# Retention block between two feed-forwards, one core: the last block in two tiles of 128 tokens, and a new order of fill and drain

## The reference, cut to what matters

```python
x = x + 0.5 * ffn(layernorm(x))          # FFN1
x = x + retention(layernorm(x))          # RET, 8 heads of 32, chunks of 64 in the reference
x = x + 0.5 * ffn(layernorm(x))          # FFN2

def ffn(x):                              # x_prev is x moved down by one token
    xr = mu_r * x + (1 - mu_r) * x_prev
    xk = mu_k * x + (1 - mu_k) * x_prev
    r = sigmoid(xr @ W_r.T)
    return r * (square(relu(xk @ W_k.T)) @ W_v.T)

def retention(x):                        # per head, state S carried from chunk to chunk
    q, k, v = x @ Wq, x @ Wk, x @ Wv
    o = ((q @ k.T) * D) @ v + (q * decay_q) @ S
    S = decay_s * S + (k * decay_k).T @ v
    return concat_heads(o) @ Wo
```

## Time and profile before

| | us |
|---|---|
| median of 3 runs | 339.76 |
| lowest, highest | 339.11, 339.87 |
| the profiled execution | 338.8 |
| its span, first to last instruction | 336.9 |

### The profile page before, as it was taken

How to read it: one execution, slowest core, us unless ns; L and a number is a source line. 1 busy time by engine, 2 the same in 40 slices (tenths; PEclk the granted TensorE clock), 3 DMA queues, 4 the chain that set the end, 5 groups by cost and what they waited for, 6 DMA issues and landing times.

```text
span 336.9 us, 11291 instructions
## 1 busy us (share of the span) xinstructions
PE 322.3 (96%) x4260; PEld 302.4 (90%) x4260; DVE 297.0 (88%) x696; ACT 210.5 (62%) x422; POOL 135.1 (40%) x242
## 2 busy tenths in 40 slices
PE   4979999999999999999999999999999999999975
PEld 4869899999999999999899999989999998989874
DVE  4989899999999999899999989999897979888954
ACT  2877556775757586674758567475857555374362
POOL 4386165608163451706245270715424154221130
PEclk9999999999999999999999999999999999999999
DMA  7610010102001020201102020100000010000001
GB/s 232 247 35 31 4 34 0 34 5 62 4 2 63 2 65 3 65 2 27 41 3 64 2 63 2 53 16 32 2 19 17 2 35 7 26 4 31 34 2 62
DMA packets 11556, 12.08 MB, mean 36 GB/s; under 512 B 1008, under 2 KB 11120, under 8 KB 11504
## 3 DMA queue, kind: packets, MB, share of 16 engines
q1 hardware_dynamic: 11072, 11.18, 10.4%
q10 hardware_dynamic: 432, 0.20, 0.2%
HBM read 7.18 MB, written 4.19 MB: 34 GB/s over the span
## 4 chain that ended last, share of the span: by engine, by line
PE 88%; DVE 4%; issue 3%; ACT 2%; POOL 1%; DMA 1%; ACTq 0%; DVEq 0%; POOLq 0%
PE psum L964 39%; PE psum L956 24%; PE psum L948 7%; PE psum L1035 5%; PE psum L1067 5%; PE psum L1054 3%; PE psum L1025 2%; PE psum L1080 2%; PE psum L1157 1%; DMA ident<-in_ident 1%; ACT xn L344 1%; DVE stats L624 1%; PE psum L1161 1%; PE psum L1127 1%; PE psum L1115 0%
## 5 line engine op out<-in xcount | busy, mean ns | idle before, releaser
L199 POOL TENSOR_TENSOR xr_lo<-xrT,xr_hi 128x512 fp32r<-128x512 f32 x24 | 41.1, 1728 | 99.8 <-ACT xr_hi L375 99.8
L344 ACT ACTIVATE xn<-x,shift,rstd 128x256 f32<-128x256 f32 x96 | 52.0, 591 | 10.1 <-POOL shift L283 10.1
L692 DVE TENSOR_TENSOR attn<-psum,decay 128x512 f32<-128x512 f32 x64 | 42.4, 683 | 4.7 <-PE psum L1035 4.7
L964 PE MATMUL psum<-w_hi,xr_hi 128*128 128x256 f32 x124 | 38.6, 312 | 1.7 <-DVE xr_lo L199 1.2
L624 DVE BATCH_NORM_STATS2 stats<-x 128x6 f32<-128x256 f32 x96 | 35.7, 414 | 4.9 <-DMA x<-in_x 4.6
L276 POOL TENSOR_TENSOR var_eps<-moments,eps 128x2 f32<-128x2 f32 x48 | 18.9, 395 | 43.7 <-DVE moments L628 42.9
L964 PE MATMUL psum<-w_hi,ka_hi 128*128 128x256 f32 x120 | 35.7, 297 | 0.7 <-ACT rgate L403 0.7
L956 PE MATMUL psum<-xa_hi,w_hi 128*128 128x256 f32 x128 | 35.8, 280 | 0.0
L956 PE MATMUL psum<-xk_hi,w_hi 128*128 128x256 f32 x120 | 34.5, 288 | 1.1 <-POOL xk_lo L193 0.9
L956 PE MATMUL psum<-xa_lo,w_hi 128*128 128x256 f32 x128 | 35.5, 278 | 0.0
L956 PE MATMUL psum<-xa_hi,w_lo 128*128 128x256 f32 x128 | 35.5, 277 | 0.0
(11 more groups left out here) (105 smaller groups left out, 1043.4 us busy)
## 6 DMA issues: line engine op xcount, KB each, us to landing
x<-in_x SPq DMA_DIRECT2D x15, 256.0 KB, 2.9
x_out<-y SPq DMA_DIRECT2D x15, 256.0 KB, 3.1
w_f<-in_w SPq DMA_DIRECT2D x7, 256.0 KB, 5.9
decay<-in_decay SPq DMA_DIRECT2D x1, 512.0 KB, 6.6
decq<-in_decq SPq DMA_DIRECT2D x1, 256.0 KB, 6.1
deck<-in_deck SPq DMA_DIRECT2D x1, 256.0 KB, 6.2
x_out<-y SPq DMA_DIRECT2D x2, 128.0 KB, 1.8
x<-in_x ACTq DMA_DIRECT2D x1, 128.0 KB, 2.8
```

Source lines behind the costliest of these rows:

```text
L199: engine.tensor_tensor(xr_lo[f][n % 2][:], xrT[f][n % 2][:], xr_hi[f][n % 2][:].bitcast(F32), ALU.subtract).then_inc(xr_lo_ready[f], 1)
L344: act.activation(xn[s][n % 2][:, t, :], x[n % len(x)][:, t, :], ACT.Identity, bias=shift[s][n % 2][:, t:t + 1], scale=rstd[s][n % 2][:, t: ...
L692: dve.tensor_tensor(attn[r][:], bank[B_SCORES[r]].rearrange("p (g c i) -> p g c i", g=G, c=TILES), decay[:, r, :, :].unsqueeze(2).broadcas ...
L964: mm = pe.matmul(halves(b)[:, t, :], xt[:, g, cols], wt[:, g, :], start=(j == 0), stop=(j == 5))
```

## The change

**Last block.** Block 15's work from its head outputs to its store is done in two tiles of 128 tokens, each with functions of its own on every engine (names that end in `_tile`). No operand is split there: `o_tile` copies the heads to an fp32 `o_last`, and all products are fp32 matmuls from `w_f32`. Each tile has a PSUM bank of its own for each product. The normalising is done on VectorE in one operation, (x - mean) x rstd, so that GpSimd only has the power left. The signals are counted per tile.

**First block.** The normalising of block 0's FFN1 (`FAST`) goes the same way: `var_eps` and the normalising are on VectorE, `minus_mean` and `shift` are gone. `split_high(W_K)` is on ScalarE, at the place of that normalising. `warm_up` multiplies a tile of zeros that GpSimd sets first, where it transposed the identity after its load.

**Order.** Fill and drain are written in another order on all engines, and some splits and adds change engine; the ten rounds are as before. Banks of block 0's and block 15's parts are others.

```diff
+        B_Y_TILE, B_T_TILE, B_HID_TILE, B_GATE_TILE, B_OUT_TILE = (3, 5), (0, 1), (2, 6), (7, 6), (7, 4)
...
+        FAST = {(FFN1, 0)}
...
             def inverse_std(s, n):
                 m = moments[s][n % 2]
-                pool.wait_ge(moments_ready[s], 2 * n + 2)
-                pool.tensor_tensor(var_eps[s][n % 2][:], m[:, :, 1], eps[:], ALU.add).then_inc(var_ready[s], 1)
-                pool.tensor_tensor(minus_mean[s][n % 2][:], m[:, :, 0], minus_one[:], ALU.mult).then_inc(minus_mean_ready[s], 1)
+                if (s, n) not in FAST:
...
+            pool.memset(zeros[:], 0.0).then_inc(zeros_set, 1)
...
+            def o_tile(t):
+                act.wait_ge(inter_done, LAST + 1)
+                act.wait_ge(intra_done, LAST + 1)
+                act.activation(o_last[:, :, tile(t)], psum[:, B_OT:B_OT + G, tile(t)], ACT.Copy).then_inc(o_hi_ready, 1)
...
+            def normalize_fast(s, n, x):
+                dve.wait_ge(rstd_ready[s], n + 1)
+                dve.wait_ge(xnT_psum[s], max(n - 1, 0))
+                for t in range(TILES):
+                    dve.tensor_scalar(xn[s][n % 2][:, t, :], x[n % len(x)][:, t, :], moments[s][n % 2][:, t, 0:1],
+                                      rstd[s][n % 2][:, t:t + 1], ALU.subtract, ALU.mult).then_inc(xn_ready[s], 1)
...
+            def mix_k_tile(t):
+                f, k = FFN2, LAST % 2
+                dve.wait_ge(d_ready[FFN2], LAST + t + 1)
+                dve.wait_ge(xk_lo_ready[f], LAST - 1)
+                for g in range(G):
+                    dve.scalar_tensor_tensor(out=xkT[f][k][:, g, tile(t)], in0=dT[f][k][:, g, tile(t)], scalar=mu[:, 1, g:g + 1],
+                                             in1=xnT[f][k][:, g, t * P:(t + 1) * P], op0=ALU.mult, op1=ALU.add).then_inc(xk_ready[FFN2], 1)
...
+            def rows_tile(b, x, w, t, done):
+
+                for g in range(G):
+                    mm = pe.matmul(halves(b)[:, t, :], x[:, g, tile(t)], w_f32[w][:, g, :], start=(g == 0), stop=(g == 1))
+                mm.then_inc(done, 1)
+
+            def retention_out_tile(t):
+                pe.wait_ge(o_hi_ready, LAST + t + 1)
+                rows_tile(B_Y_TILE[t], o_last, W_O, t, y_psum)
...
             def warm_up(b, count):
-                pe.wait_ge(ident_loaded, 16)
+                pe.wait_ge(zeros_set, 1)
                 for _ in range(count):
-                    pe.transpose(bank[b][:, 0:P], ident[:], ident[:])
+                    pe.matmul(bank[b][:, 0:P], zeros[:], zeros[:], start=True, stop=True)
...
             pe.wait_ge(attn_ready[1], 16)
             hidden(FFN2, 14, 0)
             hidden(FFN2, 14, 1)
             pe.wait_ge(gated[FFN2], 14)
             gate(FFN2, 14, 0)
-            keep_warm(3, 18)
+            gate(FFN2, 14, 1)
             pe.wait_ge(xnT_ready[FFN2], 15)
-            transpose_T(FFN2, 15)
-            gate(FFN2, 14, 1)
+            keep_warm(B_T_TILE[0], 10)
+            transpose_tile(0)
+            pe.wait_ge(attn_ready[2], 16)
+            transpose_tile(1)
             pe.wait_ge(gate_ready[FFN2], 15)
             ffn_out(FFN2, 14, 0)
             ffn_out(FFN2, 14, 1)
             pe.wait_ge(relu_ready[FFN2], 15)
-            pe.wait_ge(o_lo_ready, 16)
-            hidden_in_parts(FFN2, 15, 0)
...
+            hidden_tile(0)
             pe.wait_ge(gated[FFN2], 15)
-            gate(FFN2, 15, 0)
-            gate(FFN2, 15, 1)
+            gate_tile(0)
+            pe.wait_ge(state_ready[0], 16)
+            hidden_tile(1)
             pe.wait_ge(gate_ready[FFN2], 16)
...
+            ffn_out_tile(0)
+            pe.wait_ge(relu_ready[FFN2], 17)
+            gate_tile(1)
+            pe.wait_ge(o_hi_ready, 17)
+            ffn_out_tile(1)
```

More of the change, by code:

```diff
@@ L182, in span, with shifts @@
             return slice(0, G) if part is None else slice(part, part + 1)
+        FAST = {(FFN1, 0)}
+        def shifts(s, n):
+            return sum((s, k) not in FAST for k in range(n))
         def splits(f, n):
@@ L796, in _ @@
-            add_retention(1)
-            add_ffn(dve, FFN1, 3)
-            layer_stats(FFN2, 1, x2)
-            layer_stats(RET, 3, x1)
+            update_state(0, 1)
+            scale_state(1, 1)
+            difference(FFN2, 0)
+            mix_k(FFN2, 0)
+            xa_low(2)
+            mix_r(FFN2, 0)
+            update_state(1, 1)
+            mix_k(FFN1, 4)
+            gate(FFN1, 3)
+            o_low(1)
+            mix_r(FFN1, 4)
+            xk_low(dve, FFN2, 0)
+            add_retention(1)
@@ L1204, in _ @@
             pe.wait_ge(key_ready, 1)
-            scores(0, 1, first=True)
+            pe.wait_ge(gated[FFN1], 1)
+            scores(0, 2, first=True)
             scores(0, 0)
-            scores(0, 3)
-            scores(0, 2, last=True)
-            value(0, 1)
+            scores(0, 1)
+            scores(0, 3, last=True)
             pe.wait_ge(xnT_ready[FFN1], 4)
             key_rows(0)
+            pe.wait_ge(relu_ready[FFN1], 2)
+            hidden(FFN1, 2, 0)
+            hidden(FFN1, 2, 1)
+            pe.wait_ge(krow_ready, 1)
+            outer(0)
             pe.wait_ge(attn_ready[2], 1)
@@ L1215, in _ @@
             gate(FFN1, 2, 0)
-            pe.wait_ge(krow_ready, 1)
-            outer(0)
+            pe.wait_ge(attn_ready[3], 1)
+            inter(0, first=True)
+            gate(FFN1, 2, 1)
+            intra(0)
+            pe.wait_ge(state_ready[1], 1)
+            transpose_T(FFN1, 4)
+            pe.wait_ge(val_ready, 1)
+            query(1, 0)
+            query(1, 1)
+            pe.wait_ge(o_lo_ready, 1)
+            retention_out(0, 0)
+            retention_out(0, 1)
             pe.wait_ge(attn_ready[0], 1)
@@ L1236, in _ @@
             key(1, 1)
+            hidden(FFN1, 3, 1)
             pe.wait_ge(q_ready, 2)
             value(1, 0)
-            value(1, 1)
             pe.wait_ge(gated[FFN1], 3)
```

665 lines of the change are left out of this document (374 added, 291 removed).

## The result

The changed kernel takes **336.03 us**, median of 4 runs (335.85 to 336.07), against 339.44 of the kernel before (338.98 to 339.87) on the same chip: ratio 0.9899, 95% interval 0.9882 to 0.9916, so 3.4 us or 1.0% faster. The forecast was 335.4, within a range of 333.5 to 337.9. The profiled execution took 336.06 with a span of 334.3; that of before 338.8 and 336.9. In the spans the gain is 2.6 us, because the profiled execution of before was one of its quicker ones (a likely cause is under `tail_only_waits`).

The account below looks back on a forecast made before the run. TensorE is gapless in the middle, so gains come only from fill, gaps after 270 us and the last block's chain: 1.3 + 0.6 + 2.4 = 4.3 us, from a median of 339.76 to 335.4, range 333.5 to 337.9.

Parts of the forecast that it names:

- Part 1: Fill: first retention transpose at 21.6 against 24.33, lead 2.7 us; net gain 1.3 us, from 0.5 to 2.0.
- moved `hidden(FFN1, 2)`: Fill: 12 matmuls now behind the first retention transpose, 1.42 us to take off the lead of 2.7.
- no TensorE wait over 0.3 us from there to 270: Sign for the fill: from the first retention transpose up to 270 us TensorE never waits over 0.3 us.
- Part 2: From 270 to 315 us: TensorE's wait for `relu` goes, gain 0.6 us, from -0.4 to 0.6.
- Part 3: Last block: tiles, fp32 products and shorter normalising gain 2.4 us, from 1.2 to 3.4.
- port rival: Drain: GpSimd's add of block 14 holds up VectorE's tile 1 mix, `xk` 1.1 us late, 336.5; chance 0.2.
- The 0.2 us set aside for `xk_lo(14)`: Last block: GpSimd's `xk_lo(14)` crossing VectorE's add costs 0.2 us of the 2.6 gained.
- Fill given back: TensorE waits between 25 and 62 us, for GpSimd's queue or VectorE's 0.9 us, until 1.3 is gone: 336.7; chance 0.13.
- Slower by a cold clock: Fill: warm-up on zeros does not raise the clock, first TensorE pieces 7.9 us later, about 343.3; chance 0.05.
- Tiles too small: Last block: the drain gains only about 0.8 us, time 337.0; chance 0.08.

Follow-up runs that it names:

- tail_only_waits: Kernel before's fill with the changed last 70 us, GpSimd's `xk_lo` of block 2 waiting for block 0's x add, against the kernel before: 337.18 us, ratio 0.9919.
- y_add_waits: Changed kernel, with GpSimd's y add of block 14 waiting until VectorE has mixed both tiles of block 15: 335.17 us, ratio 0.9878 to the kernel before.

## Why the prediction was right, and where it was not

**The sum.** Forecast 4.3 us, measured 3.4 by the medians and 2.6 by the spans. The time came within the range, and the last block, the largest part, came about as its walk says; but two of three parts were over-estimated, and the hit is better than the mechanism (see the last paragraph).

**Part 1, 1.3 us, measured 0.4.** Up to the first retention transpose the walk holds well: real transposes at 6.53 (6.5 forecast), fp32 hidden at 8.88 (9.3), GpSimd's four steps in 1.5 us (1.6), the transpose at 21.85 (21.6, range 20.9 to 22.4). The last figure hides a stop that the walk did not have: the pair of mixes held up by GpSimd's split put the gate at 12.29 (11.8 forecast), and without it the transpose would have come at about 20.8. The lead less the moved `hidden(FFN1, 2)` was 1.06. The step that failed is the next one: "From that transpose on I placed every TensorE step ... none comes late". The sign given for it, "no TensorE wait over 0.3 us from there to 270", failed too: there is one of 0.8 for `krow`. I had placed GpSimd's and VectorE's queues each by itself. `ka_lo` of block 3, which is now on GpSimd, met a 0.23 us scaling ahead of `krow`, and that cost 0.9 to 1.0 us. Without this one stop the fill is worth 1.4 us by the marks, about the 1.3 of the sum. VectorE's extra work was named as the narrow place; it was not the cause, since an edit that leaves the work as it is gives the 1.0 us back.

**Part 2, 0.6 us, measured 0.0.** The wait for `relu` is gone as forecast. Against it stand 0.3 us for `xa_lo`, the same stop again (I had weighed `xk_lo` of block 13 on GpSimd, and it was that of block 12), and TensorE's own time. Windows of the kernel before, then of the changed one, from `intra(12)` to `intra(15)` (span, length, PE, PEld, DVE, ACT, POOL):

```profile
263.93:314.12 50.19, 49.53 (x717) 46.36 (x716) 42.73 (x95) 26.48 (x51) 16.61 (x27) 1.00 0.06 18
```

```profile
263.49:313.72 50.23, 49.94 (x718) 46.64 (x717) 42.78 (x94) 26.33 (x50) 17.07 (x28) 1.00 0.05 18
```

For the same work TensorE is busy 0.41 us more. In the new order its groups of six or twelve matmuls start more often behind a group of another shape: at 16 places the second matmul comes 0.19 to 0.23 us behind the first instead of 0.12, at 9 places before. Seven times 0.1 us is of that size; no run tried it, so it stays an argument.

**Part 3, 2.4 us, measured 2.2, by two errors that nearly cancel.** The port rival, at a chance of 0.2, came true as written: one pair of tile mixes of over 1 us beside the `y` add, 1.05 us by the run without it (1.1 forecast). The rest was quicker than forecast by nearly as much. The walk stands on the old clock, on which `intra(15)` starts at 314.12, so I count from there. Statistics and normalising were done 8.25 us behind it (8.2 forecast). The mixes went at 0.26 us each (0.30), and hidden of tile 1 starts at 13.72; in `y_add_waits`, without the stop, at 12.72 (13.1 forecast). From there to the end of the last add it takes 4.64 us (4.8), with three of the last four TensorE pieces at 0.87 (0.95), and from that end to the end of the span 2.2 (2.3). The 0.2 us set aside for `xk_lo(14)` makes up the rest. Without the stop this part alone would be worth 3.2 us, near the top of its range of 1.2 to 3.4. I should have given the port more than 0.2: the trace of before had GpSimd getting in at 284.00, and I had weighed the rival at one place, where the changed kernel has such a meeting at four. The Trainium skill's page "SBUF — State Buffer", section "SBUF: two separate sides", gives the lock to whichever starts first. The two rows agree with an exclusive lock, but not with that order by their recorded starts: the mix of 284.00 is recorded 0.03 us ahead of GpSimd's add and waited for it, and the add that kept GpSimd out at 18.26 is recorded at 18.36, behind it.

**The rivals.** *Fill given back* came true for 0.7 of the 1.06 us, by one meeting with GpSimd and not by VectorE's load. *Slower by a cold clock* did not: the zeros raise the clock as the identity did, and even without the early warm-up the loss is about half a microsecond, where I had priced up to 7.9. In that run the clock was up again before the first fp32 matmul of real work; what a clock that stays low longer would cost, no run shows. *Tiles too small* did not either.

**The median.** The prediction added the offset of 0.96 us between the profiled execution of before and its median to the changed kernel as well. That kernel has no such offset (median 336.03, profiled execution 336.06). Without it the forecast would have been 334.5, 1.5 us too low, still inside the range. So the 335.4 lies within 0.7 of the measured time by luck: the gain was over-estimated by 1.7 us in the span, and the offset hid more than half of it. A part of the offset is perhaps the toss-up in the old fill, which the changed kernel doesn't have.
